# A transformer block in float32: table rows stored in one transfer, and the seam before attention rearranged

## The reference

```python
x = x + 0.5 * ffn(layernorm(x))       # 16 experts, top-k tokens each, plus a shared one
x = x + attn(layernorm(x))
x = x + 0.5 * ffn(layernorm(x))
# attn: 16 heads of 16 values, causal
q, k, v = x @ Wq.T + bq, x @ Wk.T + bk, x @ Wv.T + bv
q, k = rope(q), rope(k)               # x * cos + rotate_half(x) * sin
att = softmax(where(mask, q @ k.T / 4, -inf))
y = (att @ v) @ Wo.T + bo
```

## Time and profile before

| | us |
|---|---|
| median of three runs | 1656.59 |
| the profiled execution | 1659.7 |
| its span | 1658.0 |
| first FFN | 0 to about 500 |
| projections | about 500 to 622 |
| attention | 622 to about 1157 |
| second FFN | about 1157 to 1658 |

### The profile page before, as it was taken

The page is one execution under the profiler, slowest core; times in us unless marked ns, Lnnn a source line. Parts: engine busy times, 40 slices in busy tenths (PEclk is TensorE's granted clock), DMA queues, the critical chain, the costliest instruction groups (busy, mean ns, idle before and its releaser), DMA issues. The chain is left out here.

```text
span 1658.0 us, 26486 instructions
## 1 busy us (share of the span) xinstructions
PE 1519.2 (92%) x9943; PEld 1056.3 (64%) x9945; DVE 865.2 (52%) x1851; ACT 995.0 (60%) x1359; POOL 557.1 (34%) x493
## 2 busy tenths in 40 slices
PE   4999999999975869999999999997599999999996
PEld 3788888888864653333333333332478888898895
DVE  6787676676635760123022022122678767676663
ACT  7322254545414758999999999996732225544541
POOL 3000256656544772111111021110300035656644
PEclk9999999999997987999999999999699999999998
DMA  8221266666534798315126245001722126666653
GB/s 275 71 90 52 66 168 151 157 145 152 130 38 157 212 268 171 55 25 78 34 45 116 80 64 78 2 14 52 253 70 90 52 81 158 154 152 158 156 110 39
DMA packets 120752, 183.14 MB, mean 110 GB/s; under 512 B 19568, under 2 KB 83056, under 8 KB 117360
## 3 DMA queue, kind: packets, MB, share of 16 engines
q1 hardware_dynamic: 91440, 130.04, 30.3%
q0 software_dynamic: 29184, 51.40, 14.9%
HBM read 125.82 MB, written 55.57 MB: 109 GB/s over the span
## 5 line engine op out<-in xcount | busy, mean ns | idle before, releaser
L1732 ACT ACTIVATE 8035_pr<-8035_pS 128x1024 f32<-128x1024 f32 x448 | 421.4, 1079 | 13.2 <-PE 8035_pS L1653 12.1
L1683 PE MATMUL 8035_pO<-8035_pr,6201_vres 128*32 128x512 f32 x1792 | 241.2, 609 | 4.2 <-DVE 8035_tO L1757 3.4
L1653 PEld LDWEIGHTS 8035_pS<-sq_rows,sk_rows 50*128 50x128 f32 x896 | 74.7, 186 | 200.7 <-ACT 8035_pr L1732 156.0
L1653 PE MATMUL 8035_pS<-sq_rows,sk_rows 50*128 50x512 f32 x896 | 185.6, 466 | 9.7 <-PEq L1336 5.2
L1757 DVE STREAM_TRANSPOSE 8035_tO<-8035_pO 128x512 f32<-128x512 f32 (+1 forms) x33 | 23.0, 698 | 300.1 <-PE 8035_pO L1683 300.1
L171 PE MATMUL 14715_pGU<-columns_XT,weights_wts 128*128 128x512 f32 x384 | 152.8, 398 | 1.6 <-DVE columns_XT L845 1.6
L171 PE MATMUL 110_pGU<-columns_XT,weights_wts 128*128 128x512 f32 x384 | 152.8, 398 | 1.6 <-DVE columns_XT L845 1.6
L172 PE MATMUL 110_pGU<-columns_XT,weights_wts 128*128 128x512 f32 x384 | 150.1, 391 | 0.0
L172 PE MATMUL 14715_pGU<-columns_XT,weights_wts 128*128 128x512 f32 x384 | 150.1, 391 | 0.0
L173 PE MATMUL 110_pGU<-columns_XT,weights_wts 128*128 128x512 f32 x384 | 150.0, 391 | 0.0
L173 PE MATMUL 14715_pGU<-columns_XT,weights_wts 128*128 128x512 f32 x384 | 150.0, 391 | 0.0
(11 more groups left out here) (318 smaller groups left out, 3335.1 us busy)
## 6 DMA issues: line engine op xcount, KB each, us to landing
token_table<-weights_xn POOLq DMA_DIRECT2D x16, 512.0 KB, 6.3
110_raw_g<-WgT SPq DMA_DIRECT2D x16, 512.0 KB, 3.8
110_raw_u<-WuT SPq DMA_DIRECT2D x16, 512.0 KB, 3.6
110_raw_d<-WdT SPq DMA_DIRECT2D x16, 512.0 KB, 4.1
q_rows<-rows_half SPq DMA_DIRECT2D x32, 256.0 KB, 3.4
k_rows<-rows_half SPq DMA_DIRECT2D x32, 256.0 KB, 5.1
sq_rows<-q_rows SPq DMA_DIRECT2D x32, 256.0 KB
sk_rows<-k_rows SPq DMA_DIRECT2D x32, 256.0 KB
```

Of the source, the lines that this page charges most:

```text
L1653: m = t_.matmul(to[:, e, :], key, query, start=True, stop=True)
L1683: m = t_.matmul(pO[e * 32:(e + 1) * 32, off:off + wd], vres[:, (g // GB) * TPB + kt, at:at + 32], from_(e), start=n == first[j], stop=n == ...
L1732: s_exp.done(a.activation(to, pS[:, u % RING, :, :], ACT.Exp, scale=HD ** -0.5))
```

## The change

It has four parts.

- The tables are laid out anew: high lower of all 32 heads first (256 rows), then high upper, low lower, low upper. A unit of 128 partitions x 4 pieces of 512 tokens goes out in one transfer of 1 MB, its semaphore counts 16, and the halves in SBUF are one tile. A head's rows are now 4 (or 2) blocks of eight rows, 256 rows apart; `load_head` and `load_stack` read them through a view of three dimensions, in as many transfers as before.
- The rotary sums of the last unit are made by VectorE, ahead of its low halves, and no longer by GpSimd.
- VectorE's flag work stands between the low halves: the low half of unit 13, `largest` and the maximum, the low half of unit 14, the flag's three operations, the low half of unit 15.
- ScalarE makes one exponential of one value at the end of `projections`.

```diff
     def load_stack(self, eng, dst, a, head, sem):
-        tab, ds = self.qk[a], self.bass.ds
+        tab, ds, HF = self.qk[a].rearrange("(n p) s -> n p s", n=4), self.bass.ds, HD // 2
         for lo, n in ((0, 2 * HD), (2 * HD, HD)) if a == 0 else ((0, HD), (HD, 2 * HD)):
-            eng.dma_start(dst[lo:lo + n, :].bitcast(self.f32), tab[ds(head * (2 * HD), n), :]).then_inc(sem, 16)
+            eng.dma_start(dst[lo:lo + n, :].bitcast(self.f32), tab[0:n // HF, ds(head * HF, HF), :]).then_inc(sem, 16)
...
-            half = [self.rows_at(f"half{h}", [P, KS, 2, W], f32r, 16 * 1024 * h) for h in range(2)]
+            both = self.rows_at("halves", [P, KS, 2, 2, W], f32r)
+            half = [both[:, :, h, :, :] for h in range(2)]
...
-                    for part in range(2):
-                        for u in range(2):
-                            dst = self.qk[a_].rearrange("(b h r u f) s -> b r u h f s", b=B, r=2, u=2, f=HD // 2)[bb][part][u]
-                            self.s_rows[n % KS].part(sp.dma_start(dst[:, :, cc * W:(cc + 1) * W],
-                                                                  half[part][:, n % KS, u, :].bitcast(f32)), 16)
+                    dst = self.qk[a_].rearrange("(n b p) s -> b p n s", n=4, b=B)[bb]
+                    from_ = both[:, n % KS, :, :, :].rearrange("p h u w -> p (h u) w").bitcast(f32)
+                    self.s_rows[n % KS].done(sp.dma_start(dst[:, :, cc * W:(cc + 1) * W], from_))
...
                 def high(n):
-                    a.wait_ge(*s_y.at(n + 1))
+                    a.wait_ge(*(s_y.at(n + 1) if n < 2 * J - 1 else s_last_y.at(1)))
...
                 high(2 * J - 1)
+                a.activation(warm[:, :], self.eps[0:1, :], ACT.Exp)
...
-                for n in range(POOL_LOW, 2 * J):
-                    self.s_rows[n % KS].wait(v, n // KS)
-                    low(n)
+                k = (2 * J - 1) % 3
+                s_turn.wait(v, 4 * J)
+                v.tensor_tensor(turns[k][:, 0, :], turns[k][:, 0, :], turns[k][:, 2, :], ALU.subtract)
+                s_last_y.done(v.tensor_tensor(turns[k][:, 1, :], turns[k][:, 1, :], turns[k][:, 3, :], ALU.add))
+                low(POOL_LOW)
                 largest(J - 1)
                 s_norm.wait(v, J // 2)
                 s_top.done(v.tensor_reduce(top[:, :], norm[:, :], AX.X, ALU.max))
+                low(POOL_LOW + 1)
                 v.wait_ge(*s_tt.at(1))
...
                 s_flag.done(v.tensor_scalar(self.unsafe[:, :], prod[:, :], SAFE_NORMS, None, ALU.is_gt))
+                low(POOL_LOW + 2)
                 v.wait_ge(*s_flag.at(3))
...
-                for n in range(2 * J):
+                for n in range(2 * J - 1):
                     turned(n)
...
-        head, loaded = g * 4 + hh, self.s_ld[k][pair]
+        head, loaded, HF = g * 4 + hh, self.s_ld[k][pair], HD // 2
...
                 loaded.part(sp.dma_start(dst[base + lo:base + lo + n, k, pair, :].bitcast(self.f32),
-                                         self.qk[a_][head * 2 * HD:head * 2 * HD + n, :]), 16)
+                                         self.qk[a_].rearrange("(n p) s -> n p s", n=4)[0:n // HF, head * HF:(head + 1) * HF, :]), 16)
...
-            self.s_rows = [sig(f"rows_stored{k}", 64) for k in range(ROWS_RING)]
+            self.s_rows = [sig(f"rows_stored{k}", 16) for k in range(ROWS_RING)]
```

More of the change, by code:

```diff
@@ L1037, in projections @@
             best, prod = t.sb("best", [1, 2]), t.sb("prod", [1, 1])
-            zero = t.sb("zero", [B * H, 512])
+            zero, warm = t.sb("zero", [B * H, 512]), t.sb("warm", [1, 1])
             pX = t.ps("pX", [P, DC, W])
@@ L1050, in projections @@
             s_wl, s_y, s_lo = (sig("proj_pool_" + n_) for n_ in ("wl", "y", "lo"))
-            s_last = sig("proj_dve_lo")
+            s_last, s_last_y = sig("proj_dve_lo"), sig("proj_dve_y")
             POOL_LOW = 2 * J - 3
```

## The result

The changed kernel takes 1672.7 us (median of four runs, 1669.98 to 1675.62) where the kernel before takes 1655.6 beside it. The ratio is 1.0101, with a 95% interval of 1.0074 to 1.0128: 17 us slower. The prediction was 1676. The profiled execution took 1671.5 us; its span is 1669.4, against 1658.0 before.

The account below looks back on a forecast made before the run. ScalarE's exponentials were taken to bound attention, so its start decides: 20 us later, less 0.6 for the table, is 19.5; the profiled 1659.7 becomes 1679.2, the median 1676.1. Range 1651 to 1690, to hold 8 in 10.

Parts of the forecast that it names:

- Four and two engines: Head loads from the new tables: 256 KB loads run on four engines, 128 KB on two; 56 small packets instead of 264.
- 2.6 us for 64 KB: Head loads: price of 64 KB on one DMA engine, taken as 2.6 us, kept between 2.4 and 3.5.
- Queueing behind the loads: Seam before attention: stores and heads queue on the first engine; head 3 in at about 640, attention starts at 642 to 643.
- The last issue closes the seam: End of the rotation stage: SP's last store issue closes it; TensorE starts the scores 2.73 us later.
- SP stalls: Store issues at the seam: SP stalls where much is outstanding and hands over store 15 only near 640 us.
- Sums on VectorE: Last unit's rotary sums at 609.1 us: 0.61 us each, two at 1.2, at most 2.3.
- The table load: ScalarE's exponential table loads under SP's issue, not before the first real exponential: 0.6 us gained, zero if loaded again.
- Group loads stay hidden: Attention: a group's sixteen loads take 43 us on the first engine, hidden behind 66.9 us of attention per group.
- The gain of 4.1 us: Seam, if loads keep sixteen engines: 3.5 us from SP plus 0.6 from the table, median 1652.5; this rival's chance 0.16.
- The size: Whole kernel: attention starts 20 us later, less 0.6 for the table, 19.5 us slower.
- third rival: Seam: loads confined but mostly hidden if stores pass them; heads in at 625, time about 1659; chance 0.07.
- main case: Seam: loads on few engines, 10.7 us a head on the first engine; 1676 us, range 1670 to 1690, chance 0.70.

Follow-up runs that it names:

- e1: Changed kernel with each load of a head cut into its blocks of eight rows, 12 transfers per head on eight engines; ratio to before 0.9953.
- e7: Changed kernel with loads cut into pairs of blocks, six transfers per head, every load on two engines; ratio to before 1.0303.
- e5: Changed kernel with tables of all high rows, then all low; two stores a unit, six 16-row loads a head on sixteen engines; ratio to before 0.9982.
- e2: Kernel before, tables and four stores untouched, but loads read four or two eight-row blocks of different heads (wrong data); ratio to before 1.0120.
- e10: Kernel before, unchanged, run again for a second profile; no ratio given, first score at 626.20 us.
- e4: Changed kernel on the old tables, four stores a unit and old loads; VectorE sums, reordered flag and early exponential kept; ratio to before 1.0004.
- e6: Changed kernel with only group 0's heads loaded in blocks of eight rows, groups 1 to 7 on 4 and 2 engines; ratio to before 0.9960.
- e9: Kernel before with only the early exponential added behind ScalarE's last copy of the rotations; ratio to before 0.9999.
- e8: e1 without the early exponential; ratio to before 0.9965.
- e3: Kernel before with only the new table layout, single store per unit and the change's loads; ratio to before 1.0085.

## Why the prediction was right

- *Four and two engines.* Right: 56 small packets, as counted from the earlier trace rows. The rule of the Trainium skill ("DMA: Bandwidth & Descriptors", "Why a DMA increments its semaphore by 16 and not by 1"), that the number must divide the slowest dimension of both sides, gives the same, and the traces agree in each case tried: e1 with 392 packets for eight engines, the changed kernel with 56.
- *2.6 us for 64 KB.* 2.48 us at the seam by e7, and about (46.5 - 1.2) / 16 = 2.8 us while group 2 is loaded (the sixteen pieces, less 4 x 0.3 us of shift rows). 43 us had been given for that group, 46.5 were measured.
- *Queueing behind the loads.* Right in kind and order: high(14) at 614.31 (616 given), high(15) at 627.00 (629), the last store out at 636.35 (640), the first score at 638.94 (642 to 643). The 2 to 4 us by which all of them were late in the working have two causes that the trace shows. The queue begins earlier than the 585.5 us that I took: a store now is one issue of 0.37 us and head 0's loads follow it at 582.68, where they were at 586.70. And a head with a store takes 12.69 us and not 13.3. I had costed the fewer issues of mid-stage at nothing. In the profiles they are worth something: from SP's first load of x in the stage to the end of the last rotation it is 105.7 to 106.6 us in the six kernels with one store a unit, 106.9 in e5 with two, and 106.4 to 108.9 in the five profiles with four. On the average that is 1.8 us between one store and four; why isn't shown.
- *The last issue closes the seam.* Right in every kernel: from its end to the first score it is 2.6 us in the changed kernel, 2.2 in e1, 3.1 in e2, 2.5 in e10, 2.6 in e7.
- *SP stalls.* Right, with 8.62 us for one issue of 0.4. One issue for a unit was given as 0.6 us; it is 0.37 to 0.41 where nothing is queued, and its size didn't matter where much is.
- *Sums on VectorE.* 0.69 and 0.68 us, 0.61 given. Hidden by the queue; on the old tables, in e4, no gain of them can be measured either.
- *The table load.* It moved, and wasn't repeated. 0.43 us instead of 0.6.
- *Group loads stay hidden.* Right by the waits, and by e6.
- *A wrong step.* The text says that ScalarE never waits for a DMA at L1182. One profile showed that; e10 and e9 don't. The gain of 4.1 us that I gave to the change if loads kept sixteen engines leaned on it: e4, the parts of that gain which don't need the layout, measured nothing. With the single store, and with loads that queue less, e1 reached 7.7 us, e6 6.6, e8 5.8; e5 with its two stores a unit 3.0 (each by its ratio). My gain of 4.1 us lies among them, but by luck, as its terms don't add up that way: 1.8 us come before the last rotation, the term put at nothing, and from there to the first score it is 11.8 to 12.0 us in e1, e5, e6 and e8, 14.8 in e4, and 13.3, 16.2 and 17.0 with the old seam (before, e9, e10).
- *The size.* 19.5 us were given, 17 measured by the medians, and the start of attention moved by 16.6 us against the first profile. Against the mean of the three starts of the old seam (622.4, 626.2, 623.5) it is 14.9; the difference to the 17 is within the interval of 12 to 21 us. The 17 us rest on four runs of either kernel; e3, the layout alone, loses 14 us over six runs against twenty. So the 19.5 us were too many by 2 to 5.
- *A sum that doesn't fit.* The third rival lets four heads take 9.7 us each. With the 10.7 us that a head has in the main case they are in at about 629 us and not 625, and that rival's time is about 1663 us and not 1659. Nothing else was worked out from it.

## The clock inside attention

Two profiles differ by their clock where the code is the same. The table of stretches, of the changed kernel and then of e3, from 716 to 732 us (bounds, length, busy time and instructions of PE, PEld, DVE, ACT and POOL, granted clock, DMA share, GB/s):

```profile
716.00:732.00 16.00, 14.23 (x96) 4.72 (x92) 3.81 (x7) 11.31 (x12) 1.89 (x3) 0.79 0.22 88
```

```profile
716.00:732.00 16.00, 14.24 (x120) 5.52 (x112) 5.69 (x9) 13.88 (x16) 3.88 (x6) 1.00 0.24 95
```

TensorE is busy as long in both and makes fewer matmuls in the first: for 6.8 us of it the clock is 1.2 GHz, and ScalarE has 11.31 us of exponentials instead of 13.88. The 6.8 us of the changed kernel by themselves:

```profile
719.30:726.10 6.80, 6.80 (x42) 1.66 (x38) 0.38 (x1) 5.01 (x5) 0.00 (x0) 0.50 0.23 94
```

Such a dip costs 2.6 us of exponentials, or 0.38 us for a microsecond at half clock (an estimate from this one pair). The changed kernel, e2, e4 and e9 have one about 72 us after the clock's return, e7 a longer one with its wait for loads, the others none there; before it TensorE had been at full speed and busy for some 94% of the time in both kinds (67.3 of 71.7 us in the changed kernel). What sets it off stays open. With the 9 us fewer at half clock after the first score it belongs to the sum above: the kernel before had 17.8 us at half clock in attention, this one 8.7 + 6.8 = 15.5, and 521.8 and 520.2 us of attention. At 0.38 us each the 2.3 us are 0.9 of the 1.6; the rest isn't explained.

## What to carry to other kernels

Before a table is laid out anew so that stores become fewer, look at what its loads look like afterwards: the outermost count on both sides, and how many small packets a transfer leaves. A load that falls from sixteen engines to four took a group from 23 to 46.5 us and cost nothing measurable where it had time, but it stands in the same queue as the stores around it, and there whatever waits for a store pays for it. Cutting the load into its blocks kept the new layout and turned 17 us of loss into 7.7 us of gain. And a gain in front of a full queue can be worth little until the queue is shorter: e4's was not to be measured.

## What was not expected of the hardware

- A kernel with eight engines to a load did no worse than one with sixteen, though a group's loads took longer: from the first issue to the last bytes 23 us in the kernel before, 28 in e1. The stretch of one group's loads holds 392 packets of 8 KB in each kernel. By the queue's share in the view of transfers they took 16 engines x 68 us x 30.2% = 329 us of packet time in the kernel before, 16 x 45 x 29.8% = 215 us in e1 and 16 x 65 x 13.1% = 136 us in the changed kernel: 0.84, 0.55 and 0.35 us a packet. The fewer engines share a load, the less each packet takes. What they contend for, if they do, isn't shown. The queue's line of that view (packets, MB, share of sixteen engines; small packets included) is for the changed kernel, 701 to 766 us,

```profile
q1 hardware_dynamic: 448, 3.21, 13.1%
```

  and for the kernel before, 688 to 756 us,

```profile
q1 hardware_dynamic: 656, 3.21, 30.2%
```

- The length of half clock at the start of attention is 8.3 to 17.8 us, and differs between two profiles of one kernel (17.8 and 11.5).
- Loads on few engines hold up the stores behind them by the same amount each time: from one landed store to the next, with one head between them, it is 12.69 us in the changed kernel, 12.74 in e2 and 12.68 in e3 (by ScalarE's two high halves). The Trainium skill, "DMA: Bandwidth & Descriptors", "Queues, rings and completion order", says that an engine takes the descriptors of one issuing engine's ring in their order; the traces agree, in that a store waited out the head ahead of it each time.
